# VectorE scales 256 of a step's 1024 second exponentials in the form with a sum, with one number per query

## The chip, the cores and the metric

The kernel runs on one core of a Trainium2 chip. A core has TensorE (PE), VectorE (DVE), ScalarE (ACT), GpSimd (POOL) and SyncE (SP), which each work through their own list of instructions and wait for each other by semaphores. The metric is the time on the device of one execution in microseconds (us), as the median of several runs. The profile is of one execution.

## What is computed

The input X is 2 batches of 1024 tokens of width 128. After a layer norm without parameters (xn), the result is X plus a differential attention of xn plus a mixture of experts of xn. The attention has 16 heads of two 64-wide halves:

```
A1 = einsum('bhqd,bhkd->bhqk', Q1, K1) * s        # Q, K, V: projections of xn with biases
A2 = einsum('bhqd,bhkd->bhqk', Q2, K2) * s
P  = softmax(A1, axis=-1) - lam * softmax(A2, axis=-1)
O  = einsum('bhqk,bhkd->bhqd', P, V)
Y  = Ocat @ Wo + bo                               # then a layer norm with gamma, beta, times 0.2
```

The other part is a feed-forward network of width 512 with gelu and, by a gate over the batch's mean token, two of eight experts. Everything is in f32.

## The kernel before

**Tiling.** The attention is 256 steps: 2 batches x 16 heads x 8 tiles of 128 queries. A head is 8 steps. One step handles 128 queries against all 1024 keys for both halves of the head. The PE, ACT and DVE programs run two heads (16 steps) as one loop body (`attention`, `BODY`); POOL's is written out for all 256 steps. A step goes through the engines so:

1. PE makes the scores of half 0 and half 1 in two of three PSUM slots, each with three matmuls per 512 keys (high and low parts of q and k, `product`, L518).
2. DVE takes each row's negated maximum (`row_max`, L930, 128x1024), once for each half.
3. ACT makes the exponentials with the maximum as bias and their row sums on the way (`exps`, L736): e1 of half 0 in `p_mix`, e2 of half 1 in `e2_buf` (a view of `work`). Both are rings of four steps. The sums l1 and l2 go to `l_sum`.
4. DVE takes the reciprocals of both sums (`inv_sums`, L954, into `l_inv`) and makes `l1_neg` = -lam x l1 (L955), both 128 rows by one or two numbers.
5. POOL scales e2 by 1/l2 and by -lam x l1 (L428, one instruction with two operations and two numbers per partition, 128x1024), and adds it to e1 (L431, 128x1024). So `p_mix` holds l1 times P.
6. PE transposes `p_mix` in two halves of the rows (`turn`, L536), three steps later (`LAG`), ACT copies the transposed tiles out of PSUM (`evac_pt`, L749), and after every four steps PE multiplies them with V (`pv`, L550) and one block later with Wo (`out_proj`, L562).
7. DVE copies the block's output between the two (L976) and adds it to `y_acc` times 1/l1 (`add_y`, L942).

**What stands between.** In two of a head's eight steps PE projects q and k of the next head (`proj`, L472), ACT and DVE make their high and low parts (`high_part`, `low_part`, L867 and L873). In one of eight steps POOL splits the next weights (`split_w`, L336 to L343). In the first third POOL also prepares the experts' biases and weights, `set_expert`, among them L391 (128x128) and L406 (128x256), scales of one operation; L366 (128x512) and L387 (128x4) are of the same form. In the last head POOL splits the first weights of the feed-forward network, which then runs behind the attention.

**What sets the order.** The order on each engine is written by hand. PE starts the transposes of step k-3 in the middle of the scores of step k (`open_turn`, which waits for `mix_done`), so that the second half's scores of step k come out only when the mix of step k-3 is done. On DVE `inv_sums` for step k-1 stands in step k: before the first row maximum where k mod 4 is 3, between the two where it is 1, and behind the second where it is 0 or 2. POOL's scale waits for `recip_done` (both instructions of `inv_sums`), ACT's second exponential for the mix of four steps before, its first for the transposes of four steps before.

## Time and profile before

| | |
|---|---|
| median of three runs | 1203.36 us (1198.51 to 1203.72) |
| profiled execution, its own time | 1199.68 us |
| its span in the profile | 1197.9 us |
| PE busy | 1133.8 us (95%) |
| POOL busy | 1017.1 us (85%) |
| ACT busy | 953.5 us (80%) |
| DVE busy | 905.3 us (76%) |

Busy time says how long an engine had an instruction under way, not that the engine sets the time: a matmul that waits in the array's queue counts as busy, and the shares are means over stages with different limits. The attention's 256 steps lie between about 52 and 1113 us; before them stand the layer norm and V, behind them the feed-forward network. So the rows below are read by stage: how busy each engine is in it, which of them the chain that ended last runs through, and then one engine's instructions in order of time. A line "A <- B: 32.4, 48, 5.1" says that A's engine stood idle before A 32.4 us in total, 48 times, 5.1 us at the longest, until B ended.

### The profile page before, as it was taken

The page shows a single profiled execution, that of the slowest core. Times are in us where ns is not written, and L with a number is a line of the kernel's source. Part 1 is how long each engine was busy: PE and PEld are TensorE (multiplying, and loading weights), DVE is VectorE, ACT ScalarE, POOL GpSimd, SP SyncE. Part 2 cuts the span into 40 slices and gives each one's busy share as a digit, 9 for nine tenths or more (in the row PEclk, how much of TensorE's full clock was granted, in tenths as well). Part 3 has the DMA queues.
Part 4 walks back from the last instruction along what each step waited for, and adds up shares of the span by engine and source line. Part 5 has one row for each costly group of instructions (what it writes and reads, how often), then busy time and mean ns, then how long its engine had stood idle before and what let it go on. Part 6 is the DMA issues. An engine that isn't in the chain of part 4 may idle for free.

```text
span 1197.9 us, 28095 instructions
## 1 busy us (share of the span) xinstructions
PE 1133.8 (95%) x9730; PEld 762.1 (64%) x9730; DVE 905.3 (76%) x1573; ACT 953.5 (80%) x1711; POOL 1017.1 (85%) x657
## 2 busy tenths in 40 slices
PE   5899999999999999999999999999999999997998
PEld 3666666665666666666666666666666666664797
DVE  8877887777787888878788888888888878873510
ACT  3288888888888889898888888888989888884432
POOL 3599999999999999999999999999999999999000
PEclk9989999999999999999999999999999999998999
DMA  8832122221022212222221112221122222100000
GB/s 203 321 80 51 45 50 49 49 49 33 22 49 49 49 44 49 50 49 49 49 49 36 28 40 49 49 49 45 48 49 50 49 49 50 36 10 1 1 19 18
DMA packets 74134, 63.41 MB, mean 53 GB/s; under 512 B 45172, under 2 KB 63092, under 8 KB 74100
## 3 DMA queue, kind: packets, MB, share of 16 engines
q1 hardware_dynamic: 73092, 62.78, 20.9%
q8 instruction: 19, 0.31, 0.1%
q10 hardware_dynamic: 880, 0.19, 0.1%
q14 instruction: 15, 0.12, 0.0%
q0 software_dynamic: 128, 0.01, 0.0%
HBM read 19.96 MB, written 9.44 MB: 25 GB/s over the span
## 4 chain that ended last, share of the span: by engine, by line
PE 55%; POOL 19%; ACT 12%; DVE 7%; issue 6%; ACTq 0%; DMA 0%; DVEq 0%; SPq 0%; POOLq 0%
PE ps L518 18%; PE ps L550 16%; POOL p_mix L431 10%; PE ps L536 9%; ACT work L736 7%; POOL work L428 5%; PE ps L472 3%; ACT p_mix L736 3%; DVE small L930 3%; PE ps L635 3%; PE ps L562 2%; PE ps L622 2%; ACT pt L749 1%; DVE pt L886 1%; POOL w L406 1%
## 5 line engine op out<-in xcount | busy, mean ns | idle before, releaser
L930 DVE TENSOR_REDUCE small<-ps 128x1 f32<-128x1024 f32 x512 | 614.7, 1220 | 191.4 <-PE ps L518 191.4
L431 POOL TENSOR_TENSOR p_mix<-p_mix,work 128x1024 f32<-128x1024 f32 x256 | 609.1, 2379 | 21.4
L749 ACT ACTIVATE pt<-ps 128x512 f32<-128x512 f32 x512 | 306.0, 598 | 150.4 <-PE ps L536 146.6
L536 PE MATMUL ps<-ident,p_mix 64*128 64x64 f32 x4096 | 353.0, 227 | 15.7 <-POOL p_mix L431 13.4
L536 PEld LDWEIGHTS ps<-ident,p_mix 64*128 64x128 f32 x4096 | 304.4, 139 | 69.7 <-issue 53.3
L428 POOL TENSOR_SCALAR work<-work,small 128x1024 f32<-128x1024 f32 x256 | 307.4, 1201 | 33.2 <-DVE small L955 32.4
L736 ACT ACTIVATE p_mix<-ps,small 128x1024 f32<-128x1024 f32 x256 | 286.5, 1119 | 17.3 <-DVE small L930 17.3
L736 ACT ACTIVATE work<-ps,small 128x1024 f32<-128x1024 f32 x256 | 284.7, 1112 | 0.1
L550 PE MATMUL ps<-pt,v_h 128*64 128x512 f32 x1024 | 249.5, 608 | 0.7 <-ACT pt L749 0.7
L518 PE MATMUL ps<-k_hi,q_hi 64*128 64x512 f32 x512 | 228.1, 445 | 10.9 <-ACT p_mix L736 3.7
L518 PE MATMUL ps<-k_hi,q_lo 64*128 64x512 f32 x512 | 226.0, 441 | 0.0
L518 PE MATMUL ps<-k_lo,q_hi 64*128 64x512 f32 x512 | 207.4, 405 | 0.0
L518 PE MATMUL ps<-k_hi,qx_hi 64*128 64x512 f32 x512 | 197.7, 462 | 4.9 <-ACT p_mix L736 2.8
L518 PEld LDWEIGHTS ps<-k_hi,q_hi 64*128 64x128 f32 x512 | 94.9, 185 | 145.6 <-ACT p_mix L736 67.1
L518 PE MATMUL ps<-k_hi,qx_lo 64*128 64x512 f32 x512 | 164.1, 419 | 0.0
L518 PE MATMUL ps<-k_lo,qx_hi 64*128 64x512 f32 x512 | 150.9, 393 | 0.0
L550 PEld LDWEIGHTS ps<-pt,v_h 128*64 128x64 f32 x1024 | 62.4, 136 | 94.8 <-issue 93.9
L518 PEld LDWEIGHTS ps<-k_hi,qx_hi 64*128 64x128 f32 x512 | 82.4, 190 | 35.9 <-ACT work L736 21.2
L518 PEld LDWEIGHTS ps<-k_lo,qx_hi 64*128 64x128 f32 x512 | 91.7, 186 | 6.5
L518 PEld LDWEIGHTS ps<-k_hi,q_lo 64*128 64x128 f32 x512 | 94.9, 185 | 0.1
L518 PEld LDWEIGHTS ps<-k_lo,q_hi 64*128 64x128 f32 x512 | 94.6, 185 | 0.3
L518 PEld LDWEIGHTS ps<-k_hi,qx_lo 64*128 64x128 f32 x512 | 82.0, 187 | 1.0
(135 smaller groups left out, 1242.9 us busy)
## 6 DMA issues: line engine op xcount, KB each, us to landing
qx_hi<-q_hi SPq DMA_DIRECT2D x64, 256.0 KB, 3.7
qx_lo<-q_lo SPq DMA_DIRECT2D x64, 256.0 KB, 4.7
v_scratch<-pt SPq DMA_DIRECT2D x16, 512.0 KB, 4.2
v_h<-v_scratch SPq DMA_DIRECT2D x32, 256.0 KB, 3.1
wqk_raw<-in_L_attn_Wk SPq DMA_DIRECT2D x31, 64.0 KB, 1.8
wqk_raw<-in_L_attn_Wq SPq DMA_DIRECT2D x31, 64.0 KB, 1.9
wo_dup<-in_L_attn_Wo SPq DMA_DIRECT2D x2, 512.0 KB, 8.0
w_raw<-in_L_ffn_W1e SPq DMA_DIRECT2D x4, 256.0 KB, 3.2
```

Source lines behind the costliest of these rows:

```text
L428: pool.tensor_scalar(e2, e2, l_inv[:, 2 * km + 1:2 * km + 2], l1_neg[:, km % 4:km % 4 + 1], ALU.mult, ALU.mult).then_inc(scaled, 1)
L431: pool.tensor_tensor(e1, e1, e2, ALU.add).then_inc(mix_done, 1)
L472: mm = pe.matmul(into[:, half * BANK:(half + 1) * BANK], wt[:, col:col + P], a[:, bass.ds(t0 + half * BANK, BANK)], start=j == 0, stop=j == 2)
L518: return pe.matmul(slot[SLOT[k, s]][:, half * BANK:(half + 1) * BANK], (ax if half else a)[rows, q0:q0 + P], b[rows, k0 + half * BANK:k0 + ...
L536: mm = pe.transpose(pt_ps[:, c * D:(c + 1) * D], p_mix[rows, col:col + P], ident[rows, rows])
L550: mm = pe.matmul(o_ps[half * D:(half + 1) * D, :], vh4[:, (kb // 2) % 2, c, :], pt4[:, kb % 2, c, :], start=c < 2, stop=c >= KC - 2, skip_ ...
L562: mm = pe.matmul(o_ps[:, t * E:(t + 1) * E], o_t[:, col:col + P], wo_dup[:, bass.ds(head * E, E)], start=True, stop=True, skip_group_check ...
L622: mm = pe.matmul(slot[u % 3][:, half * BANK:(half + 1) * BANK], w[set_][:, c * P:(c + 1) * P], a[:, t0:t0 + BANK], start=j == 0, stop=j == 2)
L635: mm = pe.matmul(out_ps, hidden[u % 4][:, t * P:(t + 1) * P], w24[:, 0 if f == 0 else TOPK * b + f, c, :], start=i == 0 and t % 4 == 0, st ...
L736: act.activation((p_mix, e2_buf)[s][:, k % 4 * S:(k % 4 + 1) * S], slot[SLOT[k, s]], ACT.Exp, bias=neg_max[:, m:m + 1], scale=1.0, accum_o ...
L749: act.activation(pt4[:, kb % 2, :, j * P + half * D:j * P + (half + 1) * D], pt_ps.rearrange("p (c q) -> p c q", c=KC), ACT.Copy).then_inc ...
L930: dve.tensor_reduce(neg_max[:, m:m + 1], slot[SLOT[k, s]], AX.X, ALU.max, negate=True)\
```

## The change

VectorE takes the first 256 of the 1024 columns of e2 (`DVE_KEYS`) and scales them; POOL scales the other 768 and then adds all 1024 to e1, when both are done (`part_scaled` beside `scaled`). The scale becomes one number per query, -lam x l1 / l2: DVE makes it in `l1_neg` from the reciprocal of l2, l1 and -lam, in one instruction with two operations, behind a wait for the reciprocal. POOL's scale is then an instruction with one operation and one number per partition. DVE's is a multiply and an add of zero with a row sum as a second output (`accum_out` into `part_sum`), which nothing reads.

```diff
@@ -24,6 +24,7 @@
 HC = HID // P
 SETS = 1 + B * TOPK
 LAG = 3
+DVE_KEYS = 256
 BANK = 512
 UNITS = B * (1 + TOPK) * HC
 SET_MAIN = 5 + B
@@ -108,6 +109,7 @@
         al_in = small[:, 217:218]
         bias_now = [small[:, 236 + 3 * i:239 + 3 * i] for i in range(2)]
         zero, eighth = small[:, 242:243], small[:, 243:244]
+        part_sum = small[:, 244:245]
 
 
         e2_buf = work[:, :]
@@ -149,7 +151,7 @@
         v_loaded = [sem(f"v_loaded{i}") for i in range(2)]
         s_ready, max_done, exp_done = sem("s_ready"), sem("max_done"), sem("exp_done")
         recip_done = sem("recip_done")
-        scaled, mix_done = sem("scaled"), sem("mix_done")
+        scaled, part_scaled, mix_done = sem("scaled"), sem("part_scaled"), sem("mix_done")
         pt_ready, pt_evac = sem("pt_ready"), sem("pt_evac")
         pv_done, o_evac, y_mm, y_evac = sem("pv_done"), sem("o_evac"), sem("y_mm"), sem("y_evac")
         w1_split, h_mm = sem("w1_split"), sem("h_mm")
@@ -425,9 +427,10 @@
                     e1 = p_mix[:, km % 4 * S:(km % 4 + 1) * S]
                     e2 = e2_buf[:, km % 4 * S:(km % 4 + 1) * S]
                     pool.wait_ge(recip_done, 2 * n)
-                    pool.tensor_scalar(e2, e2, l_inv[:, 2 * km + 1:2 * km + 2], l1_neg[:, km % 4:km % 4 + 1],
-                                       ALU.mult, ALU.mult).then_inc(scaled, 1)
+                    pool.tensor_scalar(e2[:, DVE_KEYS:], e2[:, DVE_KEYS:], l1_neg[:, km % 4:km % 4 + 1], None, ALU.mult)\
+                        .then_inc(scaled, 1)
                     pool.wait_ge(scaled, n)
+                    pool.wait_ge(part_scaled, n)
                     pool.tensor_tensor(e1, e1, e2, ALU.add).then_inc(mix_done, 1)
                 if k % TB == SPLIT_W_AT and now(g, k, -2 * TB):
                     split_w(g * 2 + k // TB + 2)
@@ -952,8 +955,14 @@
                     dve.wait_ge(exp_done, 2 * m + 2)
                     after(dve, scaled, m - 3)
                     dve.reciprocal(l_inv[:, r:r + 2], l_sum[:, l:l + 2]).then_inc(recip_done, 1)
-                    dve.tensor_scalar(l1_neg[:, e:e + 1], l_sum[:, l:l + 1], lam_neg, None, ALU.mult)\
-                        .then_inc(recip_done, 1)
+                    dve.wait_ge(recip_done, 2 * m + 1)
+                    dve.tensor_scalar(l1_neg[:, e:e + 1], l_inv[:, r + 1:r + 2], l_sum[:, l:l + 1], lam_neg,
+                                      ALU.mult, ALU.mult).then_inc(recip_done, 1)
+
+                    part = e2_buf[:, e * S:e * S + DVE_KEYS]
+                    dve.wait_ge(recip_done, 2 * m + 2)
+                    dve.tensor_scalar(part, part, l1_neg[:, e:e + 1], 0.0, ALU.mult, ALU.add, accum_out=part_sum)\
+                        .then_inc(part_scaled, 1)
 
                 if j == 3 and now(g, k - j, 2 * QB):
                     add_y(g, kb)
```

On POOL, at the start of the steps, before (`work` is e2, `small` holds the numbers per query):

```order
L428 TENSOR_SCALAR work<-work,small 128x1024 [waits recip_done]
L431 TENSOR_TENSOR p_mix<-p_mix,work 128x1024 [waits scaled]
L428 TENSOR_SCALAR work<-work,small 128x1024 [waits recip_done]
L431 TENSOR_TENSOR p_mix<-p_mix,work 128x1024 [waits scaled]
L428 TENSOR_SCALAR work<-work,small 128x1024 [waits recip_done]
```

and after:

```order
L430 TENSOR_SCALAR work<-work,small 128x768 [waits recip_done]
L434 TENSOR_TENSOR p_mix<-p_mix,work 128x1024 [waits part_scaled,scaled]
L430 TENSOR_SCALAR work<-work,small 128x768 [waits recip_done]
L434 TENSOR_TENSOR p_mix<-p_mix,work 128x1024 [waits part_scaled,scaled]
L430 TENSOR_SCALAR work<-work,small 128x768 [waits recip_done]
```

Nothing moved on POOL; the scale is narrower, and the add waits for one semaphore more.

On DVE in a step of the loop with `inv_sums` behind a row maximum, and the block's additions to `y_acc` (L942, later L945) behind it, before (`ps` are the scores or the output in PSUM):

```order
L930 TENSOR_REDUCE small<-ps 128x1 [waits s_ready]
L163 REGISTER_ALU [waits exp_done]
L954 RECIPROCAL small<-small 128x2 [waits scaled]
L955 TENSOR_SCALAR small<-small 128x1
L942 ISA [waits y_mm]
```

and after:

```order
L933 TENSOR_REDUCE small<-ps 128x1 [waits s_ready]
L165 REGISTER_ALU [waits exp_done]
L957 RECIPROCAL small<-small 128x2 [waits scaled]
L959 TENSOR_SCALAR small<-small 128x1 [waits recip_done]
L964 TENSOR_SCALAR work,small<-work,small 128x256 [waits recip_done]
L945 ISA [waits y_mm]
```

The 128x256 multiply is inserted, and both small multiplies now wait for the instruction before them.

## Rows read from the trace of the kernel before

**Rows 1.** Windows: PE, PEld, DVE, ACT, POOL busy us (count), then clock, DMA share, GB/s
```profile
52.00:330.00 278.00, 262.96 (x2292) 170.58 (x2290) 217.44 (x367) 236.30 (x428) 265.78 (x175) 0.99 0.22 52
330.00:1000.00 670.00, 655.78 (x5881) 429.61 (x5880) 547.03 (x931) 589.03 (x1076) 630.75 (x395) 1.00 0.19 46
```

**Rows 2.** Chain that ended last, by line, in 52 to 330 and 330 to 1000 us
```profile
by line: POOL p_mix L431 38.5%; POOL work L428 19.3%; PE ps L518 8.1%; PE ps L550 5.6%; issue 4.7%; PE ps L536 4.0%; ACT work L736 2.9%; POOL w L406 2.6%; DVE small L930 2.2%; ACT p_mix L736 2.2%; POOL wqk_lo L343 1.9%; POOL x_all L377 1.8%
...
by line: PE ps L518 26.4%; PE ps L550 24.1%; PE ps L536 12.6%; ACT work L736 10.4%; issue 7.6%; PE ps L472 4.9%; ACT p_mix L736 4.1%; DVE small L930 3.9%; PE ps L562 3.6%; ACT pt L749 1.2%; ACT small L702 0.6%; ACTq L702 0.4%; ACTq L163 0.2
```

**Rows 3.** Timeline of POOL from 253 us: start us, us, instruction
```profile
253.27 1.19 POOL L428 TENSOR_SCALAR work<-work,small 128x1024 f32<-128x1024 f32 x1
254.55 2.39 POOL L431 TENSOR_TENSOR p_mix<-p_mix,work 128x1024 f32<-128x1024 f32 x1
256.93 0.91 POOL L406 TENSOR_SCALAR w<-w,small 128x256 f32<-128x256 f32 x1
257.83 1.19 POOL L428 TENSOR_SCALAR work<-work,small 128x1024 f32<-128x1024 f32 x1
```

**Rows 4.** Timeline of POOL from 608 us, then windows of L428 alone, of L336 alone
```profile
608.32 0.39 POOL L336 TENSOR_TENSOR wqk_raw<-wqk_raw,small 128x128 f32<-128x128 f32 x1
...
610.51 1.19 POOL L428 TENSOR_SCALAR work<-work,small 128x1024 f32<-128x1024 f32 x1
...
52.00:330.00 278.00, 78.99 (x66) 0.99 0.22 52
330.00:1000.00 670.00, 199.19 (x166) 1.00 0.19 46
...
330.00:1000.00 670.00, 8.53 (x21) 1.00 0.19 46
```

**Rows 5.** Groups of POOL by form: out<-in, count, busy us, mean ns, idle before
```profile
L431 POOL TENSOR_TENSOR p_mix<-p_mix,work 128x1024 f32<-128x1024 f32 x256 | 609.1, 2379 | 21.4
L428 POOL TENSOR_SCALAR work<-work,small 128x1024 f32<-128x1024 f32 x256 | 307.4, 1201 | 33.2 <-DVE small L955 32.4
...
L406 POOL TENSOR_SCALAR w<-w,small 128x256 f32<-128x256 f32 x8 | 7.3, 914 | 0.0
...
L391 POOL TENSOR_SCALAR b_bc<-b_bc,small 128x128 f32<-128x128 f32 x4 | 2.4, 602 | 0.0
...
L366 POOL TENSOR_SCALAR w<-w,small 128x512 f32<-128x512 f32 x1 | 1.6, 1550 | 0.0
...
L387 POOL TENSOR_SCALAR small<-small 128x4 f32<-128x4 f32 x1 | 0.3, 298 | 0.0
```

**Rows 6.** Waits of POOL for DVE: us in total, times, longest
```profile
POOL work L428 <- DVE small L955: 32.4, 48, 5.1
```

**Rows 7.** Timeline of POOL: its first scale with the wait before, its last add
```profile
52.63 1.19 POOL L428 TENSOR_SCALAR work<-work,small 128x1024 f32<-128x1024 f32 x1 [5.05 <-DVE small L955]
...
1104.90 2.35 POOL L431 TENSOR_TENSOR p_mix<-p_mix,work 128x1024 f32<-128x1024 f32 x1
```

**Rows 8.** DVE and ACT: two lines' durations min/median/max, groups, two timeline rows
```profile
L843 DVE TENSOR_SCALAR p_mix<-x_all,small x16: 335/341/943, 8.1 to 20.3; 128x128 f32<-128x128 f32 x16
...
L955 DVE TENSOR_SCALAR small<-small x256: 192/195/199, 52.3 to 1099.4; 128x1 f32<-128x1 f32 x128
...
L736 ACT ACTIVATION_READ_ACCUMULATOR work<-ps,small 128x1 f32 x256 | 51.1, 200 | 0.0
...
609.46 0.16 DVE L954 RECIPROCAL small<-small 128x2 f32<-128x2 f32 x1
609.52 0.20 DVE L955 TENSOR_SCALAR small<-small 128x1 f32<-128x1 f32 x1
...
L930 DVE TENSOR_REDUCE small<-ps 128x1 f32<-128x1024 f32 x332 | 398.1, 1220 | 115.1 <-PE ps L518 115.1
```

**Rows 9.** Windows with PE's gaps, columns as in rows 1
```profile
60.00:75.00 15.00, 13.20 (x108) 10.37 (x109) 10.31 (x17) 13.14 (x25) 12.94 (x9) 0.77 0.70 147
...
1090.00:1100.00 10.00, 6.28 (x44) 3.86 (x44) 4.51 (x13) 5.75 (x11) 9.76 (x7) 0.83 0.00 0
```

## The prediction

> **What bounds the kernel now.** I read the windows by stage first, then the chain of waits by line in the same two stages, then GpSimd's (POOL's) own timeline, because POOL is where the change takes work away. From 52 to 330 us POOL is busy 265.78 of 278 us and the chain that ended last runs through it: 38.5% on the add at L431 and 19.3% on the scale at L428 [rows 1, 2]. From 330 to 1000 us TensorE (PE) is busy 655.78 of 670 us, and the chain runs through PE, ScalarE's (ACT's) exponentials and VectorE's (DVE's) row maxima; POOL is not among its larger parts [rows 1, 2]. But POOL is only just off the chain there. In its timeline a step is one scale and one add back to back: starts 253.27, 254.55, 256.93, so 1.28 us from scale to add and 2.38 us from add to the next instruction, 3.66 us a step [rows 3]. The weight split once per eight steps takes from 608.32 to 610.51, 2.19 us [rows 4]. The stage from 330 to 1000 us holds 166 steps (the scale's count) and 21 splits [rows 4]: 166 x 3.66 + 21 x 2.19 = 654 us of POOL work in 670 us. So the pace of 670 / 166 = 4.04 us a step leaves POOL about 0.1 us a step. Whatever makes POOL's step longer by more than that sets the time of the whole attention part.
>
> **POOL's scale: the form changes, and that costs more than the columns save.** The change hands POOL 768 columns instead of 1024, and turns the instruction from one with two operations (times one number, times another) into one with a single operation. The trace has the first form at one size: 128x1024, 1201 ns, 256 of them [rows 5]. It has the single-operation form at four smaller sizes, on the same engine: 128x4 in 298 ns, 128x128 in 602 ns, 128x256 in 914 ns, 128x512 in 1550 ns [rows 5]. These lie on a line: from 256 to 512 columns (1550 - 914) / 256 = 2.48 ns a column, from 128 to 256 (914 - 602) / 128 = 2.44 ns. A 512-column instruction of this form already takes longer than the 1024-column one with two operations. The eight at 914 ns stand in the middle of the steady work, right between an add and a 1.19 us scale [rows 3], so neither the start of the program nor a different neighbour explains them. Carried on from 512 to 768 columns: 1550 + 256 x 2.484 = 2186 ns. Against 1201 ns that is +985 ns a step, 256 steps, +252.2 us of POOL work. The bounds: 1550 + 256 x 2.44 = 2175 ns below (-3 us in all), and 1550 x 768 / 512 = 2325 ns above, if nothing of the row were fixed (+36 us in all). I take 2186 ns, since the fixed part shows in the 298 ns of four columns.
>
> The bound from the other form: through its 1201 ns at 1024 columns and the 298 ns at four columns there are 0.885 ns a column, and 768 columns would take 298 + 764 x 0.885 = 974 ns, 227 ns less than now. That is the rival below. 
> **What of it is absorbed.** POOL waits now, for DVE's scale number (L955), 32.4 us in 48 places; 5.05 us of that lie before its first scale at 52.63 us [rows 6, 7], which leaves 27.3 us. With a longer POOL step these waits go: the number is waiting before POOL asks. PE's order lets the scores run ahead by three steps of mixes, and after a mix has ended POOL still has a whole step queued, 3.66 us now and 3.66 + 0.99 = 4.65 us then, while the chain from that mix through the scores, one row maximum (1.22 us [rows 8]), the reciprocal and the scale number has to be back. I leave 2 us of waits at the start.
>
> **DVE's added work lies beside that.** Per step it gets a 128x256 multiply with a sum, and two waits on its own results, and loses nothing. Nearest rows: a 128x1 multiply takes 195 ns and a 128x128 one 341 ns [rows 8], 1.15 ns a column, so 256 columns cost about 341 + 128 x 1.15 = 488 ns. Now the second small instruction starts 0.06 us after the first [rows 8]; made to wait for it, and the multiply for that one, the three take about 0.16 + 0.20 + 0.49 us and perhaps 0.1 us for the waits, 0.95 us where the two took 0.26 us: +0.7 us a step. A separate read of the sum, not shown for DVE here, could make that 0.9 us, by ACT's read of its own accumulator, 200 ns [rows 8]. Behind it on DVE's queue stand the next row maximum, and in some steps the low parts of q or k and the copy of the output block. From 330 to 1000 us DVE waits for PE 115.1 us before its row maxima [rows 8], 0.69 us a step at 4.04 us a step. At POOL's new pace (next paragraph) a step has 0.88 us more room, so DVE at 547.03 / 166 = 3.3 us [rows 1, 4], and 4.0 us with the 0.7 us, of 4.9 us is covered: cost nothing. If that cover were gone, the whole 0.7 us would be exposed to PE. POOL's add waits for DVE's quarter as well; DVE starts it on the same number that starts POOL's scale and needs 0.5 us against 2.19 us. Cost nothing.
>
> **The sum.** POOL's new step is 3.66 + 0.985 = 4.65 us, plus 2.19 / 8 = 0.27 us for the split, 4.92 us against the present pace of 4.04 us. POOL stays saturated from its first scale to its last add. The stretch behind the last add (it ends at 1104.90 + 2.35 = 1107.25 us [rows 7], 90.6 us before the span's end) does not change. Span: 1197.9 + 252.2 - 27.3 + 2 = 1424.8 us. The profiled execution took 1199.68 us, 1.8 us over its span, and the median of the three runs lies 3.7 us above it; with both, 1430 us.
>
> **Rivals.** (a) *The form doesn't matter on POOL* and 768 columns take 974 ns. Then POOL has 58 us less to do and leaves the chain. *Faster:* the stage from 52 to 330 us goes from 278 / 66 = 4.21 us [rows 4] to 4.04 us a step, -11 us, and DVE's addition hides wholly in its waits: 1192 us. This case decides itself at DVE's gap, and holds only if its +0.7 us a step falls wholly into the 0.69 us that it waits. (b) *The same, but DVE becomes the bound:* its three instructions stand ahead of a row maximum in half of the steps and behind the second in the others, so I take half of 0.7 us as exposed, 256 x 0.35 = +90 us, -11 us: 1282 us. For (a) and (b) speaks only that the two-operation form is not in the trace at a small size; against them speak 14 single-operation instructions of four sizes on one line [rows 5].
>
> (c) *PE's clock falls.* At POOL's pace PE idles about a sixth of the time. The granted clock was 0.77 from 60 to 75 us, where PE was busy 13.20 of 15 us, and 0.83 from 1090 to 1100 us, where it was busy 6.28 of 10 us; in the two long stages it was 0.99 and 1.00 [rows 1, 9]; a mean below 1 is a mixture of the two levels, 2.4 and 1.2 GHz. PE needs at most 4.04 us a step at full clock, so a mean below 4.04 / 4.92 = 0.82 makes it the bound. At 0.77 it would be 5.25 us a step, +0.33 x 256 = +84 us: 1514 us. Against it: at 0.83 POOL was busy 9.76 of 10 us [rows 9], and as soon as PE is late it has no gaps.
>
> (d) *DVE's multiply blocks POOL* for its 0.49 us, +125 us: 1555 us. No two such instructions overlap in this trace. In a sentence by itself: the Trainium skill, "SBUF — State Buffer", Who interferes with whom, holds that VectorE and GpSimd share a pair of ports and that a multiply which writes out its accumulator doesn't take it, which would make the blocking nil; no row of before tests that.
>
> **How the numbers follow.** The forecast with its own bounds has a chance of 0.80, (b) 0.08, (a) 0.04, (c) 0.05, (d) 0.03. Range of the forecast: below, 1430 less 3 for the rate, a few us for waits and 20 us for a stage after the last add that begins with less queued, so 1400; above, plus 36 us for the rate bound and up to 14 us of waits that stay (half of the 27 us), 1480. (a), (b) and (d) and most of (c) stay outside, together just under 0.2. A measurement of this kernel can tell about 0.5% from no change. Slower by more: all of (b), (c), (d) and the forecast, and less a little for (b) ending near zero, 0.94; faster, most of (a), 0.03; the same, 0.03.
>
> **What would show it.** In the profile after: POOL's scale at 128x768 near 2186 ns (right) or under 1000 ns (then (a) or (b)); POOL busy over 97% from 60 us on, and its starts 4.65 us apart; the chain of waits running through the scale and the add in all of the attention part; DVE's waits for PE longer, not shorter; DVE's new multiply near 0.49 us, and POOL's add still at 2379 ns (if longer, (d)); the granted clock above 0.82. The prediction is wrong if the scale's duration follows the columns alone.

## The result: 1424.8 us, 18.6% slower

| | before | changed |
|---|---|---|
| median | 1202.21 us (1198.51 to 1203.72, 4 runs) | 1424.76 us (1424.12 to 1424.82, 4 runs) |
| profiled execution, own time | 1199.68 us | 1424.72 us |
| its span | 1197.9 us | 1422.9 us |
| GpSimd (POOL) busy | 1017.1 us (85%) | 1270.5 us (89%) |
| TensorE (PE) busy | 1133.8 us (95%) | 1205.8 us (85%) |

The ratio of the times is 1.186, 95% interval 1.183 to 1.188. The lines of the changed kernel stand 2 to 9 lower in its code: POOL's scale is L430, its add L434, VectorE's (DVE's) row maximum L933, its reciprocal L957, its number per query L959, its new multiply L964.

The engines by windows of the changed kernel (PE, PEld, DVE, ACT, POOL busy us with counts, then clock, DMA share, GB/s), to be held against [rows 1]:

```profile
52.00:330.00 278.00, 227.56 (x1895) 145.13 (x1893) 215.35 (x412) 199.08 (x356) 270.04 (x142) 0.96 0.19 47
330.00:1230.00 900.00, 775.72 (x6478) 502.12 (x6474) 714.70 (x1387) 663.42 (x1184) 879.39 (x438) 0.94 0.16 38
```

POOL is busy 97.7% of the long stage (94% in [rows 1]); PE, which was busy 98% there, is down to 86%. The chain that ended last, from 330 to 1200 us, says the same; in [rows 2] the chain of that stage ran through PE, ACT and DVE:

```profile
by line: POOL work L430 44.2%; POOL p_mix L434 38.3%; issue 11.8%; POOL wqk_lo L345 2.2%; POOL wqk_hi L342 1.8%; POOL wqk_raw L338 0.9%; POOL w L408 0.2%; POOLq L433 0.2%; PE ps L539 0.1%; PE ps L521 0.1%; DVE small L959 0.1%; POOLq L341 0.
```

The groups of POOL and DVE (count, busy us, mean ns of one, idle before), which answer to [rows 5, 8]; the profile calls DVE's multiply with a sum TENSOR_SCALAR_CACHE_REDUCE and shows the read of the sum as an instruction of its own:

```profile
L434 POOL TENSOR_TENSOR p_mix<-p_mix,work 128x1024 f32<-128x1024 f32 x256 | 607.4, 2373 | 21.4
L430 POOL TENSOR_SCALAR work<-work,small 128x768 f32<-128x768 f32 x256 | 564.5, 2205 | 5.8 <-DVE small L959 5.6
...
L933 DVE TENSOR_REDUCE small<-ps 128x1 f32<-128x1024 f32 x512 | 620.9, 1222 | 254.0 <-PE ps L521 251.9
L964 DVE TENSOR_SCALAR_CACHE_REDUCE work<-work,small 128x256 f32<-128x256 f32 x256 | 122.7, 479 | 9.1
L959 DVE TENSOR_SCALAR small<-small 128x1 f32<-128x1 f32 x256 | 69.8, 273 | 9.4
...
L964 DVE DVE_READ_ACCUMULATOR work<-work,small 128x1 f32 x256 | 21.3, 83 | 0.0
```

The scale of 768 columns takes 2205 ns where that of 1024 took 1201 ns [rows 5]. The add is as it was. POOL waits for DVE 5.6 us in all (32.4 us in [rows 6]), 5.25 us of it before its first scale. In order of time its steps follow each other with under 0.1 us of idle between two instructions, 4.65 us from scale to scale:

```profile
53.59 2.20 POOL L430 TENSOR_SCALAR work<-work,small 128x768 f32<-128x768 f32 x1 [5.25 <-DVE small L959]
...
800.02 2.20 POOL L430 TENSOR_SCALAR work<-work,small 128x768 f32<-128x768 f32 x1
802.31 2.38 POOL L434 TENSOR_TENSOR p_mix<-p_mix,work 128x1024 f32<-128x1024 f32 x1
804.67 2.20 POOL L430 TENSOR_SCALAR work<-work,small 128x768 f32<-128x768 f32 x1
...
1331.95 2.39 POOL L434 TENSOR_TENSOR p_mix<-p_mix,work 128x1024 f32<-128x1024 f32 x1
```

The last add ends at 1334.3 us, 88.6 us before the span's end (90.6 us before the change, [rows 7]).

### The profile page after: what moved, and what is told of

Read it like the earlier page. It is cut to its first block, busy times and chain, and to the rows that moved or that the text cites. A ratio compares the mean times of both kernels' runs of the same rounds, so it can differ in the third digit from the quotient of the medians.

```text
span 1422.9 us, 28877 instructions
## 1 busy us (share of the span) xinstructions
PE 1205.8 (85%) x9730; PEld 799.3 (56%) x9730; DVE 1064.7 (75%) x2085; ACT 971.9 (68%) x1711; POOL 1270.5 (89%) x657
## 4 chain that ended last, share of the span: by engine, by line
POOL 77%; issue 11%; PE 8%; DVE 3%; ACT 1%; DMA 0%; POOLq 0%; DVEq 0%; SPq 0%; ACTq 0%
POOL work L430 38%; POOL p_mix L434 33%; PE ps L638 3%; PE ps L625 2%; POOL wqk_lo L345 2%; POOL wqk_hi L342 2%; PE ps L502 1%; POOL wqk_raw L338 1%; DVE pt L889 1%; PE ps L521 1%; PE ps L553 1%; PE ps L539 0%; DVE small L933 0%; POOL x_all L379 0%; PE ps L460 0%
## 5 line engine op out<-in xcount | busy, mean ns | idle before, releaser
L933 DVE TENSOR_REDUCE small<-ps 128x1 f32<-128x1024 f32 x512 | 620.9, 1222 | 254.0 <-PE ps L521 251.9
L434 POOL TENSOR_TENSOR p_mix<-p_mix,work 128x1024 f32<-128x1024 f32 x256 | 607.4, 2373 | 21.4
L430 POOL TENSOR_SCALAR work<-work,small 128x768 f32<-128x768 f32 x256 | 564.5, 2205 | 5.8 <-DVE small L959 5.6
L539 PE MATMUL ps<-ident,p_mix 64*128 64x64 f32 x4096 | 370.0, 233 | 178.1 <-POOL p_mix L434 172.8
L539 PEld LDWEIGHTS ps<-ident,p_mix 64*128 64x128 f32 x4096 | 310.1, 145 | 269.1 <-issue 265.0
L553 PE MATMUL ps<-pt,v_h 128*64 128x512 f32 x1024 | 252.2, 614 | 0.7 <-ACT pt L752 0.7
L521 PE MATMUL ps<-k_hi,q_hi 64*128 64x512 f32 x512 | 234.0, 457 | 16.3 <-DVE k_lo L876 6.9
L521 PE MATMUL ps<-k_hi,q_lo 64*128 64x512 f32 x512 | 237.1, 463 | 0.0
L521 PE MATMUL ps<-k_lo,q_hi 64*128 64x512 f32 x512 | 217.8, 425 | 0.0
L521 PE MATMUL ps<-k_hi,qx_hi 64*128 64x512 f32 x512 | 190.8, 464 | 3.6 <-ACT p_mix L739 2.7
L521 PE MATMUL ps<-k_hi,qx_lo 64*128 64x512 f32 x512 | 158.9, 413 | 0.0
L964 DVE TENSOR_SCALAR_CACHE_REDUCE work<-work,small 128x256 f32<-128x256 f32 x256 | 122.7, 479 | 9.1
```

The lines of the kernel that those rows point to most:

```text
L430: pool.tensor_scalar(e2[:, DVE_KEYS:], e2[:, DVE_KEYS:], l1_neg[:, km % 4:km % 4 + 1], None, ALU.mult)\
L434: pool.tensor_tensor(e1, e1, e2, ALU.add).then_inc(mix_done, 1)
L521: return pe.matmul(slot[SLOT[k, s]][:, half * BANK:(half + 1) * BANK], (ax if half else a)[rows, q0:q0 + P], b[rows, k0 + half * BANK:k0 + ...
L539: mm = pe.transpose(pt_ps[:, c * D:(c + 1) * D], p_mix[rows, col:col + P], ident[rows, rows])
L553: mm = pe.matmul(o_ps[half * D:(half + 1) * D, :], vh4[:, (kb // 2) % 2, c, :], pt4[:, kb % 2, c, :], start=c < 2, stop=c >= KC - 2, skip_ ...
L933: dve.tensor_reduce(neg_max[:, m:m + 1], slot[SLOT[k, s]], AX.X, ALU.max, negate=True)\
```

## Experiments: is it the form?

Two theories. Theory 1: GpSimd's scale with one operation is slow by its form, and all else is a term beside it. Theory 2: the form is innocent, and the size, the start inside the buffer or DVE's new work beside it costs. Two kernels separate them from both ends: the slow form at the old size, and the fast form at the new size. Edits are against the changed kernel unless said otherwise.

**one_op_1024.** DVE's share is taken out, the number per query stays:

```diff
-DVE_KEYS = 256
+DVE_KEYS = 0
...
-                    pool.wait_ge(part_scaled, n)
...
-                    part = e2_buf[:, e * S:e * S + DVE_KEYS]
-                    dve.wait_ge(recip_done, 2 * m + 2)
-                    dve.tensor_scalar(part, part, l1_neg[:, e:e + 1], 0.0, ALU.mult, ALU.add, accum_out=part_sum)\
-                        .then_inc(part_scaled, 1)
```

> GpSimd scales all 1024 columns, by the one number per query, in the form with one operation; VectorE scales nothing, and GpSimd's add waits for no second semaphore. The output stays the reference's. Theory 1 (the form is what costs): GpSimd's scale takes 1550 + 512 x 2.484 = 2822 ns against 1201 ns in the form with two operations at the same size, the mean distance from one scale to the next grows from 3.66 to 5.28 us, and the time is 1202 + 256 x 1.62 - 27 = 1590 us. Theory 2 (the form is innocent; the 768 columns, their start inside the buffer, or VectorE's new instruction beside them cost): the scale takes 1201 ns as before and the time stays at 1202 us within 1%.

Measured: 1585.33 us, ratio 1.321 (1.315 to 1.326). Its scale, by form:

```profile
L430 POOL TENSOR_SCALAR work<-work,small 128x1024 f32<-128x1024 f32 x256 | 728.5, 2846 | 5.2 <-DVE small L958 5.2
```

2846 ns against 1201 ns at the same 1024 columns, in the same buffer, with nothing of DVE's beside it. Theory 2 falls: the size, the offset and DVE's multiply are all absent, and the cost is there. Theory 1's 2822 ns and 1590 us were off by 1% and 0.3%.

**two_op_ptr.** The other way round: everything of the change stays, and POOL gets its second operation back. `one` is a column of ones that POOL fills once at the start.

```diff
-                    pool.tensor_scalar(e2[:, DVE_KEYS:], e2[:, DVE_KEYS:], l1_neg[:, km % 4:km % 4 + 1], None, ALU.mult)\
+                    pool.tensor_scalar(e2[:, DVE_KEYS:], e2[:, DVE_KEYS:], l1_neg[:, km % 4:km % 4 + 1], one,
+                                       ALU.mult, ALU.mult)\
```

> As the changed kernel, with VectorE's 256 columns in the form with a sum, but GpSimd scales its 768 columns in the form with two operations and two numbers per partition, the second a column of ones. Theory 1: the scale falls to about 974 ns (298 ns for four columns and 0.885 ns for each further one), GpSimd leaves the chain, and the time is between 1192 us (VectorE's additions all in its waits) and 1282 us (half of them exposed). Theory 2: the scale stays at 2204 ns and the time at 1425 us.

**two_op_imm.** The same with `1.0` in place of the column `one`.

> As two_op_ptr, but the second operation multiplies by an immediate 1.0. Theory 1 as it stands (a second operation that is no bypass is what makes it fast): about 974 ns a scale and the time of two_op_ptr. If instead two numbers per partition are what makes it fast: the scale stays at about 2204 ns and the time at 1425 us. Theory 2: 2204 ns as well, but then in two_op_ptr too.

Measured: 1229.18 us for two_op_ptr, ratio 1.025 (1.021 to 1.029), and 1228.67 us for two_op_imm, ratio 1.0235 (1.019 to 1.028). Their scales, first two_op_ptr:

```profile
L431 POOL TENSOR_SCALAR work<-work,small 128x768 f32<-128x768 f32 x256 | 252.8, 987 | 116.4 <-DVE small L961 116.2
```

and two_op_imm:

```profile
L430 POOL TENSOR_SCALAR work<-work,small 128x768 f32<-128x768 f32 x256 | 233.4, 912 | 135.4 <-DVE small L960 135.2
```

A multiplication by one, added to the instruction, takes it from 2205 to 912 ns and the kernel from 1424.8 to 1228.7 us. It needn't be a second number per partition; an immediate does, and is 75 ns faster. So of the 222.6 us between the medians some 196 us are the form. The rest is 27 us by these medians, and 30 us by the seven runs of before that were timed together with two_op_ptr and two_op_imm (median 1198.85 us). It is still there when POOL is fast, and the idle time before the scale names whom POOL now waits for: DVE, 116 and 135 us.

**ruler.** The kernel before, and behind POOL's last add 35 more instructions: seven forms at 64, 256, 512, 768 and 1024 columns, each waiting for the one before.

```diff
+            for cols in (64, 256, 512, 768, 1024):
+                t = work[:, 0:cols]
...
+                        i = pool.tensor_scalar(t, t, eighth, None, ALU.mult)
...
+                        i = pool.tensor_scalar(t, t, eighth, eighth, ALU.mult, ALU.mult)
...
+                        i = pool.tensor_scalar(t, t, eighth, 1.0, ALU.mult, ALU.mult)
```

> The kernel before, with 35 more GpSimd instructions behind its last add, in a stretch where GpSimd is idle for 90 us: 64, 256, 512, 768 and 1024 columns, each as one operation with a number per partition; two operations with two such numbers; two with a number and an immediate 1.0 (times, times); one with an immediate; two with a number and an immediate 0.0 (times, plus); two immediates; and a multiply of two tensors with one number spread over the columns. The output is the reference's, the time that of before plus nothing (1199 us; the extra work is about 50 us of 90). Theory 1: every form with one operation lies on 280 ns + 2.48 ns a column, every form with two on about 300 + 0.88 ns a column or a little less with immediates, whatever the operations; the two-tensor multiply on 190 + 1.67 ns. If the size decides instead, the one-operation form at 1024 falls to 1201 ns.

Measured: 1203.8 us in one run (before 1199.33 us, up to 1203.86). Its timeline of POOL; L454 is one operation with a number per partition, L456 two operations with two such numbers, L458 a number and an immediate 1.0:

```profile
1111.18 0.93 POOL L454 TENSOR_SCALAR work<-work,small 128x256 f32<-128x256 f32 x1
1112.21 0.55 POOL L456 TENSOR_SCALAR work<-work,small 128x256 f32<-128x256 f32 x1
1112.85 0.48 POOL L458 TENSOR_SCALAR work<-work,small 128x256 f32<-128x256 f32 x1
...
1123.64 2.21 POOL L454 TENSOR_SCALAR work<-work,small 128x768 f32<-128x768 f32 x1
1125.95 0.98 POOL L456 TENSOR_SCALAR work<-work,small 128x768 f32<-128x768 f32 x1
1127.02 0.90 POOL L458 TENSOR_SCALAR work<-work,small 128x768 f32<-128x768 f32 x1
...
1141.85 1.97 POOL L458 TENSOR_SCALAR work<-work,small 128x1024 f32<-128x1024 f32 x1
```

From 256 to 768 columns: one operation (2207 - 926) / 512 = 2.50 ns a column, two operations (976 - 549) / 512 = 0.83 ns, a factor of three. The two-operation lines start somewhat higher or lower by their operands (549 and 479 ns at 256 columns); the one-operation form starts with a disadvantage of 121 ns at 64 columns (433 against 312 ns) and loses 1.67 ns with each further column. Times and plus with an immediate 0.0 took the same 481 ns at 256 and 692 ns at 512 columns as times and times, so which operation comes second is not what matters.

The rows from about 1130 us on do not belong to these lines: 1.97 us at 1024 columns for the form that takes 1126 ns in the steady work of other kernels here. In that stretch DVE runs instructions with two inputs in SBUF, some of which get longer as well:

```profile
1136.61 2.84 POOL L454 TENSOR_SCALAR work<-work,small 128x1024 f32<-128x1024 f32 x1
1139.56 2.19 POOL L456 TENSOR_SCALAR work<-work,small 128x1024 f32<-128x1024 f32 x1
...
1138.20 1.22 DVE L1039 TENSOR_TENSOR y_acc<-y_acc,small 128x1024 f32<-128x1024 f32 x1
1139.46 1.22 DVE L1039 TENSOR_TENSOR y_acc<-y_acc,gb_bc 128x1024 f32<-128x1024 f32 x1
1140.72 2.10 DVE L1039 TENSOR_TENSOR y_acc<-y_acc,x_all 128x1024 f32<-128x1024 f32 x1
1142.86 2.03 DVE L1039 TENSOR_TENSOR y_acc<-y_acc,small 128x1024 f32<-128x1024 f32 x1
```

In the kernel before, where POOL has nothing to do then, all six of these DVE instructions take the same time:

```profile
1137.61 1.23 DVE L1017 TENSOR_TENSOR y_acc<-y_acc,small 128x1024 f32<-128x1024 f32 x1
```

In the ruler the ends alternate from 1140.68 us on: DVE at 1140.68, POOL 1141.75, DVE 1142.82, POOL 1143.82, DVE 1144.89, each 1.0 to 1.1 us behind the other engine's. That looks like taking turns, since each needs 1.1 to 1.2 us when it is alone; no run was made to test it. It is not so for every pair: POOL's one-operation scale at 1136.61 us and DVE's instruction at 1138.20 us lie side by side and neither is longer than alone.

So for the three forms shown the ruler is good up to 768 columns, and for 1024 the steady rows of one_op_1024 and number_only stand.

## Experiments: what DVE's share costs and gives

With POOL's form mended the change is still 2.5% slower than before. Theory D says that DVE's queue in front of its row maxima is what costs; theory L that the number reaches POOL later. Three kernels with POOL in the fast form (immediate 1.0) take the share apart.

**number_only.** As one_op_1024, with the second operation:

```diff
-                    pool.tensor_scalar(e2[:, DVE_KEYS:], e2[:, DVE_KEYS:], l1_neg[:, km % 4:km % 4 + 1], None, ALU.mult)\
+                    pool.tensor_scalar(e2[:, DVE_KEYS:], e2[:, DVE_KEYS:], l1_neg[:, km % 4:km % 4 + 1], 1.0,
+                                       ALU.mult, ALU.mult)\
```

> The one number per query alone: VectorE makes it behind a wait for the reciprocal and scales no columns; GpSimd scales all 1024 in the form with two operations, the second times an immediate 1.0 (the output is the same). Theory D (what costs in two_op_ptr is VectorE's queue: 0.78 us more a step in front of its row maxima): only about 0.2 us of that is left, so 30 us x 0.2 / 0.78 = +8 us, less up to 5 us where GpSimd's scale is shorter by the 75 ns seen at 768 columns (66 steps of the first stage): 1198 to 1207 us. Theory L (what costs is that the number reaches GpSimd 0.2 us later, GpSimd's waits for it having grown from 32 to 116 us): all of the loss stays, 1225 to 1230 us.

Measured: 1195.03 us, ratio 0.996 (0.9945 to 0.998). That is 4.3 us faster than the runs of before beside it (1199.33 us), and 3 us below the range that theory D gave. Its groups, and its windows (columns as in [rows 1]):

```profile
L430 POOL TENSOR_SCALAR work<-work,small 128x1024 f32<-128x1024 f32 x256 | 288.9, 1128 | 47.6 <-DVE small L959 46.6
...
L933 DVE TENSOR_REDUCE small<-ps 128x1 f32<-128x1024 f32 x512 | 614.3, 1220 | 159.4 <-PE ps L521 159.4
...
52.00:330.00 278.00, 265.96 (x2330) 171.76 (x2327) 230.59 (x371) 239.01 (x434) 264.78 (x177) 0.99 0.23 55
330.00:1000.00 670.00, 655.68 (x5888) 430.27 (x5886) 567.96 (x930) 589.87 (x1079) 618.75 (x395) 1.00 0.19 45
```

The scale is 73 ns shorter than the form with two numbers per partition (1201 ns), 19 us over all 256 steps. Over the 67 steps of the first stage it is 5 us, and about that much is gained. The matmuls done by 330 us say the same: 2330 against 2292 before, 38 more or 4.5 us of the stage, while the long stage has 5888 against 5881. So POOL's relief counts where POOL paces, here about a quarter of it. DVE's longer way to the number costs nothing that shows, so theory L falls as the cause of the 30 us.

**dummy_part.** DVE does its share on a spare buffer of 256 columns, filled with ones at the start; POOL scales all 1024 columns itself, in the form with two operations, and doesn't wait for DVE's multiply. DVE's multiply waits for its own of the step before, a wait that two_op_imm doesn't have.

```diff
+        spare = sb("spare", 256)
...
-                    part = e2_buf[:, e * S:e * S + DVE_KEYS]
+                    part = spare[:, :]
+                    after(dve, part_scaled, m)
...
-                    pool.wait_ge(part_scaled, n)
```

> VectorE's share without GpSimd's relief: VectorE makes the number and multiplies 256 columns of a spare buffer in the form with a sum, GpSimd scales all 1024 columns in the form with two operations (immediate 1.0) and waits for no share of VectorE. Theory D: VectorE's queue is as long as in two_op_imm, so at least its 1229 us; GpSimd's 200 ns more a step count only where it paces, 66 steps in the first stage if at all: 1229 to 1242 us. If GpSimd's relief is worth what it saves (0.21 us a step over all 256): 1229 + 55 = 1284 us.

Measured: 1242.62 us, ratio 1.036 (1.033 to 1.040), just over the upper end of what theory D allowed. So DVE's work costs without any part of POOL's: 1242.6 - 1195.0 = 47.6 us. Not all of that is the multiply's length, though, for in dummy_part it also starts later. Number and multiply in two_op_imm, then in dummy_part:

```profile
612.16 0.27 DVE L960 TENSOR_SCALAR small<-small 128x1 f32<-128x1 f32 x1
612.47 0.48 DVE L965 TENSOR_SCALAR_CACHE_REDUCE work<-work,small 128x256 f32<-128x256 f32 x1
...
611.51 0.27 DVE L962 TENSOR_SCALAR small<-small 128x1 f32<-128x1 f32 x1
611.90 0.48 DVE L968 TENSOR_SCALAR_CACHE_REDUCE spare<-spare,small 128x256 f32<-128x256 f32 x1
```

From start to start it is 0.39 us in place of 0.31 us, 0.08 us a step; over the run DVE is idle before the multiply 30.8 us in place of 9.1 us. The edits leave two reasons for it, the wait more and the other buffer. The 14 us between dummy_part and two_op_imm can therefore be this delay, or POOL's relief (912 for 1126 ns, 55 us of POOL time), or both. The matmuls speak for the delay as a good part of it: from 52 to 330 us dummy_part has 2256 against 2293, 37 fewer or 4.5 us, but from 330 to 1000 us, where POOL is not on its chain, 5590 against 5648, 58 fewer or 7 us. What is shown is the net cost of the share, multiply and relief together: 1228.7 - 1195.0 = 34 us. The multiply alone costs between 34 and 48 us.

Windows of two_op_imm show what took POOL's place, and so does its chain from 330 to 1000 us, where DVE's row maximum has 12.2% (3.9% in [rows 2]) and POOL is not among the larger parts:

```profile
52.00:330.00 278.00, 259.92 (x2293) 171.40 (x2292) 255.54 (x501) 237.37 (x427) 247.23 (x176) 0.99 0.22 52
330.00:1000.00 670.00, 629.75 (x5648) 414.77 (x5644) 618.88 (x1209) 574.68 (x1036) 559.48 (x378) 1.00 0.19 44
...
by line: PE ps L522 22.4%; issue 16.6%; DVE small L934 12.2%; PE ps L554 11.6%; PE ps L540 9.6%; PE ps L566 5.2%; DVE y_acc L946 4.7%; DVE k_lo L877 4.2%; DVE q_lo L871 3.8%; DVE small L960 3.8%; DVE work L965 2.3%; DVE small L958 1.2%; DVE
```

DVE is busy 92% of both stages, where it was 78% and 82% [rows 1], and it waits for PE before its row maxima 36.0 us in the second, where it waited 115.1 us [rows 8]. POOL falls from 94% to 84% and PE does fewer instructions in the same 670 us (5648 against 5881). The load has moved from an engine with 6% to spare to one whose spare time lay in pieces between its row maxima.

**keys_128.** two_op_imm with `DVE_KEYS = 128`.

> As two_op_imm, with VectorE scaling 128 columns instead of 256 and GpSimd 896 in the form with two operations. Theory D: VectorE's multiply falls from 479 to about 346 ns, GpSimd's scale rises to about 1018 ns. From number_only (1195 us) to dummy_part (1243 us) 0.56 us a step on VectorE cost 48 us, a third of its 143 us; from dummy_part to two_op_imm GpSimd's relief of 214 ns a step gave back 14 us. So 0.13 us less a step gives back 11 us and half the relief takes 7 us: 1229 - 11 + 7 = 1225 us, 1215 to 1229. If the instruction's place in the queue costs and not its length: 1229 to 1236 us. If only length did: 1195 + 17 = 1212 us.

Measured: 1211.54 us, ratio 1.009 (1.006 to 1.012). DVE's multiply took 346 ns and POOL's scale 1018 ns, both as worked out. The time missed the estimate (1225 us, 1215 to 1229) and came out at the 1212 us that the expectation's last sentence gives, half of the way from 0 to 256 columns. With 0, 128 and 256 columns the times are 1195, 1212 and 1229 us, 17 us for each 128; the three were not timed together, and with each held against its own runs of before the steps are 15 and 19 us. So it goes by the columns about evenly, but not by DVE's time: the first 128 columns put 0.35 us and their wait on DVE, the second 128 only 0.13 us. The estimate took the loss as proportional to DVE's time, and it is not. DVE's waits for PE before its row maxima fall from 159.4 us (0 columns) to 86.8 (128) and 63.3 us (256): the first columns mostly fill gaps, the second find fewer. That fits, but POOL's share of the columns changes too between these kernels, and no run holds it still.

**no_sum.** The changed kernel with DVE's multiply in the plain form:

```diff
-                    dve.tensor_scalar(part, part, l1_neg[:, e:e + 1], 0.0, ALU.mult, ALU.add, accum_out=part_sum)\
+                    dve.tensor_scalar(part, part, l1_neg[:, e:e + 1], None, ALU.mult)\
```

> As the changed kernel, with GpSimd's scale of one operation, but VectorE scales its 256 columns in the plain form without a sum. By theory 1 GpSimd still sets the pace: if the two engines don't hinder each other, 1425 us, with VectorE's multiply at most at its 479 ns. If they do, GpSimd's scale or add, or VectorE's multiply, gets longer than 2204, 2373 and 479 ns; at one multiply of 0.3 to 0.5 us a step that GpSimd has to wait out the time is 1425 + 256 x 0.3 to 0.5 = 1502 to 1553 us. Apart from that: the Trainium skill, SBUF - State Buffer, section Who interferes with whom, holds that a multiply without a sum takes the ports that GpSimd needs and that whoever comes first keeps them for the whole instruction.

**no_sum_two_op.** The same edit in two_op_imm.

> As two_op_imm, but VectorE's 256 columns in the plain form without a sum, which took 1014 ns on average in no_sum against 479 ns. There VectorE had room; here it has not. Theory D: +0.53 us a step on VectorE, exposed nearly in full: 1229 + 0.8 x 136 = 1338 us, 1310 to 1365. If GpSimd's shorter work leaves VectorE's multiply at 700 ns or less: 1229 + 0.22 x 256 = 1285 us. If VectorE's queue is not the bound: 1229 us.

Measured: no_sum 1429.78 us, 5.0 us over the changed kernel; no_sum_two_op 1334.32 us, ratio 1.113 (1.110 to 1.115), 106 us over two_op_imm. DVE's multiply in no_sum, durations min/median/max:

```profile
L964 DVE TENSOR_SCALAR work<-work,small x256: 352/768/2539, 52.8 to 1330.4; 128x256 f32<-128x256 f32 x128
```

and in no_sum_two_op:

```profile
L965 DVE TENSOR_SCALAR work<-work,small x256: 352/380/2371, 52.9 to 1234.7; 128x256 f32<-128x256 f32 x128
```

Undisturbed it is faster than the form with a sum, 352 against 479 ns (whose min/median/max are 478/479/482). But it can last 2539 ns, 2187 ns more, and POOL's scale takes 2205 ns. In order of time, from no_sum, a long one ends just behind the instruction of POOL in which it starts, here at 605.27 us behind 605.12 us:

```profile
604.40 0.87 DVE L964 TENSOR_SCALAR work<-work,small 128x256 f32<-128x256 f32 x1
...
602.74 2.38 POOL L434 TENSOR_TENSOR p_mix<-p_mix,work 128x1024 f32<-128x1024 f32 x1
```

It is no single case. Of the multiplies longer than 0.6 us between 60 and 1220 us that can be held against an instruction of POOL, all 117 in no_sum_two_op and 153 of 162 in no_sum end 0.13 to 0.16 us behind that instruction of POOL. So DVE's multiply waits for it and isn't slowed evenly.

On average it takes 1014 ns in no_sum, where DVE has room, and 852 ns in no_sum_two_op, where it has none. POOL waits too, but less: its scale takes 2226 ns in no_sum (2205 with the sum) and 1007 ns in no_sum_two_op (912 with the sum). In no_sum, where POOL paces, those 21 ns over 256 steps are the 5 us; the 1502 to 1553 us that the expectation gave for the case that POOL waits out DVE's multiply did not come. In no_sum_two_op the expectation's total (1338 us) was met with another sum: DVE's multiply is 0.37 us a step longer, not 0.53, and the 106 us are 0.41 us a step. How much of that is DVE's delay and how much POOL's 0.1 us a step, the runs don't part. The Trainium skill, "SBUF — State Buffer", Who interferes with whom, has this rule: the plain multiply can take the ports that it shares with GpSimd, and whoever comes first keeps them for the whole instruction, while the form that writes out its accumulator does not take them. Both halves agree with these runs: 352 to 2539 ns for the one form, 478 to 482 ns for the other.

The trace of the kernel before held a sign of it. In [rows 8] a plain multiply of DVE (L843) has a median of 341 ns and a maximum of 943 ns, and at 15 us a small one that took 172 ns at 6.75 us ends with POOL's instruction beside it, at 16.2 us:

```profile
14.98 1.21 DVE L834 TENSOR_SCALAR small<-small 128x8 f32<-128x8 f32 x1
...
13.79 2.38 POOL L417 TENSOR_TENSOR k_lo<-w_raw,k_hi 128x1024 fp32r<-128x1024 f32 x1 [4.29 <-ACT k_hi L692]
```

## Experiment: a version faster than both

**fast_forms.** number_only, with every other scale of one operation on POOL given a second one, and three two-tensor forms with a constant spread over the columns written as times a constant, times 1.0:

```diff
-                pool.tensor_tensor(wqk_hi[:, :], wqk_raw[:, :], zero.to_broadcast([P, W_COLS]), ALU.subtract)\
+                pool.tensor_scalar(wqk_hi[:, :], wqk_raw[:, :], 1.0, 1.0, ALU.mult, ALU.mult)\
...
-                    pool.tensor_scalar(w2[:, cols], w2[:, cols], coef[:, s_:s_ + 1], None, ALU.mult)\
+                    pool.tensor_scalar(w2[:, cols], w2[:, cols], coef[:, s_:s_ + 1], 1.0, ALU.mult, ALU.mult)\
```

> number_only, with every scale of one operation on GpSimd (experts' biases and weights) given a second operation times 1.0, and the weight split's first two instructions and the feed-forward weights' high part, two-tensor forms with a constant spread over the columns, written as times a constant, times 1.0. The output is the reference's. GpSimd paces only the first 67 steps and the last few: there 8 x 0.44 + 4 x 0.25 us for the experts, 8 x (0.26 + 0.11) us for the splits, about 7.5 us, and 5 x 0.42 = 2.1 us at the end: 1195 - 9 = 1186 us if GpSimd's time counts in full there, 1190 us if half of it, 1195 us if GpSimd's relief is worth nothing.

Measured: 1187.57 us, ratio 0.988 (0.986 to 0.991). Its groups:

```profile
L342 POOL TENSOR_SCALAR wqk_hi<-wqk_raw 128x320 fp32r<-128x320 f32 x31 | 14.3, 460 | 5.0 <-POOL wqk_raw L338 5.0
...
L409 POOL TENSOR_SCALAR w<-w,small 128x256 f32<-128x256 f32 x8 | 3.8, 480 | 0.0
```

460 for 720 ns and 480 for 914 ns. The gain over number_only is 7.5 us by the medians and 9 us when each is held against its own runs of before (1200.85 and 1199.33 us), so most or all of the 9 us. It comes where POOL paces, as the windows of PE show: 2386 matmuls from 52 to 330 us against 2330 in number_only, 56 more or 6.5 us of the stage, and about as many in the stage from 330 to 1000 us (5874 against 5888):

```profile
52.00:330.00 278.00, 269.78 (x2386) 176.72 (x2383) 233.13 (x377) 243.10 (x442) 262.01 (x180) 0.99 0.24 57
330.00:1000.00 670.00, 655.46 (x5874) 429.74 (x5872) 568.98 (x935) 590.58 (x1078) 612.49 (x395) 1.00 0.18 44
```

## Why the prediction was right

The forecast was 1430 us, with a range of 1400 to 1480 us; measured 1424.8 us.

| step of the sum | predicted | measured |
|---|---|---|
| POOL's scale, 768 columns, one operation | 2186 ns, +252.2 us | 2205 ns, +257.0 us |
| POOL's waits that go | -27.3 + 2 us | from 27.3 to 0.4 us behind the first scale |
| POOL from scale to scale | 4.65 us | 4.65 us |
| behind the last add | 90.6 us | 88.6 us |
| DVE's multiply | 488 ns, covered | 479 ns and 83 ns for reading the sum, covered |
| span | 1424.8 us | 1422.9 us |
| span to median | 1.8 + 3.7 us | 1.8 us and nothing |

**The form's price** was read off 14 instructions that the kernel had anyway [rows 5], and carried from 512 to 768 columns. It was 19 ns short a step, 4.9 us in all. The shorter stretch behind the last add (2.0 us) and nearly 5 us of other small terms go the other way, among them 1.7 us of shorter adds (2373 for 2379 ns) and 1.6 us of waits that I had left in and that went. So part of the closeness of the span, 1.9 us, is luck of terms that cancel.

**The last term was mis-sized.** I added the 3.7 us by which the median of before lay above its profiled run. The changed kernel doesn't have that spread: its four runs lie within 0.7 us, those of before within 5.2 us. That explains most of the miss of 5.2 us. The runs on record show what the spread goes with. Of the twelve runs of before that were timed beside keys_128, the three with a granted clock of 0.984 took 1205.0 to 1205.2 us and the four at 0.991 to 0.993 took 1197.2 to 1199.1 us. With POOL as the pace there is no such tie: one_op_1024 took 1585.27 us at a clock of 0.893 and 1585.38 us at 0.929. So the term belonged to a kernel that PE paces, and it should have been nothing. That the clock is what makes the spread of before is read from this tie; no run tested it.

**DVE's cover** was right, with the parts off in both directions. The number per query takes 273 ns (195 ns before, and it is two operations on numbers per partition now), the multiply 9 ns less than estimated. The separate read of the sum exists and takes 83 ns, but it starts together with the next row maximum (both at 800.33 us), so it doesn't hold that up. DVE waits for PE 251.9 us where it waited 191.4 us on the page of before: its work is there, and its gaps grew more.

**Rivals (a) and (b)**, that the form doesn't matter, are wrong for the change as written. As a forecast for the fast form they were right in kind and off in size: two_op_ptr lies at 1229 us, between (a)'s 1192 and (b)'s 1282 us. The step of (b) that fails is "half of 0.7 us exposed", 0.35 us a step: the number costs nothing that shows, and the multiply costs 34 us net of POOL's relief, 0.13 us a step, or 0.19 us at most (dummy_part).

**Rival (c), the clock.** The granted clock did fall, to 0.94 in the long stage and 0.87 from 1230 to 1333 us:

```profile
1230.00:1333.00 103.00, 82.72 (x645) 51.49 (x644) 69.12 (x142) 64.61 (x116) 100.76 (x52) 0.87 0.06 14
```

PE stood idle before its transposes for POOL's mixes 172.8 us over the whole span, and a mean below 1 means that for part of the time it ran at the lower of the two levels. It stayed above the 0.82 at which PE would have become the bound, and POOL waited 0.4 us in all behind its first scale. What it costs is nil here, which the two runs of one_op_1024 above show as well: 4% of the clock apart, 0.1 us apart in time.

**Rival (d), blocked ports.** DVE's multiply with a sum lasts 478 to 482 ns over all 256, and POOL's add 2373 ns (2379 before): neither waits for the other. For the plain form the rival was real, but it is mostly DVE that waits: in no_sum POOL's scale gets 21 ns longer and not 490 ns.

## What to carry to other kernels

Before an instruction changes its form, look in the trace for the same form at any size on the same engine; an instruction with one operation less can be three times slower, and the rows that say so may lie in a corner of the kernel where they cost nothing. Work taken from an engine that is 94% busy is worth only what that engine paces: of the 19 us that number_only took off POOL, 4.3 us came out, about a quarter. The engine that takes work over pays in front of whatever waits behind it. And when a control kernel has one wait more than the kernel it is held against, look up in the trace what it costs: here the multiply starts 0.08 us later in each step, which leaves the worth of POOL's relief open. An elementwise instruction given to DVE beside a busy GpSimd goes in the form with a sum, which is slower by itself (479 against 352 ns) and doesn't wait for GpSimd.

## What I had not expected of the hardware

On GpSimd a multiply by a number with a second multiply by 1.0 behind it takes 0.83 ns a column and without it 2.50 ns, from 256 to 768 columns; the size of the factor, and that an immediate second number is enough and 73 to 75 ns faster than one per partition, were new. DVE's separate read of the sum takes 83 ns, less than half of ScalarE's 200 ns [rows 8]. And near 1141 us of the ruler a GpSimd scale took 1973 ns for 1126, while DVE's two-input instructions beside it took 2.0 to 2.1 us for 1.22 us, their ends alternating as if they took turns. No stretch of the steady work shows it, since DVE has no instruction with two SBUF tensors there.
